# Row maxima of the attention stage: two parts in an even stream of one pair of tiles per half-step, with one VectorE instruction over both heads where their banks are neighbours

## The reference

```
std_attn = softmax(mask(q @ k.T * dh**-0.5))        # "dot" logits, per head
geo_attn = softmax(mask(read_lines @ J_write.T * inc_scale))   # "geo" logits, 6 components per head
combined = (1 - gate) * (std_attn @ v) + gate * (geo_attn @ geo_v)
x = layernorm(x + combined @ out_w + out_b)
x = layernorm(x + down(silu(gate_proj(x)) * up_proj(x)))
```

## Time and profile before

| | |
|---|---|
| median of 3 runs | 1913.83 us (1912.52 to 1914.31) |
| the profiled execution | 1911.92 us, of which span 1910.2 us |
| PE busy | 1686.7 us (88%) |
| ACT busy | 1218.8 us (64%) |
| VectorE (DVE) busy | 1057.9 us (55%), of it 487.9 us in 768 full maxima |
| mean granted TensorE clock | 0.944 of 2.4 GHz |

### The profile page before, as it was taken

How to read it: one execution, slowest core, us unless ns; L and a number is a source line. 1 busy time by engine, 2 the same in 40 slices (tenths; PEclk the granted TensorE clock), 3 DMA queues, 4 the chain that set the end, 5 groups by cost and what they waited for, 6 DMA issues and landing times. The chain is left out here.

```text
span 1910.2 us, 36280 instructions
## 1 busy us (share of the span) xinstructions
PE 1686.7 (88%) x11793; PEld 606.2 (32%) x11793; DVE 1057.9 (55%) x2509; ACT 1218.8 (64%) x1457; POOL 336.5 (18%) x478
## 2 busy tenths in 40 slices
PE   7887469679999999999989999999999874999998
PEld 4544112122222222222222222222222222565555
DVE  4775586355755657556565565755756103545432
ACT  3553308568888788887878878888888861211221
POOL 4432402012111111111111111111110213112000
PEclk9998659889999999999999999999999987999999
DMA  5774511112211111111120111111102004232000
GB/s 170 215 216 145 164 62 41 63 45 77 87 44 67 44 61 73 42 61 57 51 86 34 67 45 59 73 42 62 71 33 68 18 25 152 72 101 97 11 22 22
DMA packets 97400, 140.67 MB, mean 74 GB/s; under 512 B 8144, under 2 KB 66320, under 8 KB 95152
## 3 DMA queue, kind: packets, MB, share of 16 engines
q1 hardware_dynamic: 96000, 135.08, 20.6%
q0 software_dynamic: 624, 2.75, 0.4%
q10 hardware_dynamic: 576, 0.28, 0.1%
HBM read 81.96 MB, written 55.61 MB: 72 GB/s over the span
## 5 line engine op out<-in xcount | busy, mean ns | idle before, releaser
L1074 ACT ACTIVATE prob<-ex 128x1024 f32<-128x1024 f32 (+1 forms) x1152 | 1050.2, 978 | 276.9 <-PE ex L915 256.0
L1101 DVE TENSOR_REDUCE mp<-mx 128x1 f32<-128x512 f32 x768 | 487.9, 685 | 170.2 <-PE mx L943 170.2
L988 PE MATMUL pv<-prob,va 128*32 128x512 f32 (+3 forms) x5120 | 581.1, 545 | 0.6 <-POOL prob L887 0.6
L887 POOL TENSOR_SCALAR_AFFINE_SELECT prob<-prob 128x256 f32<-128x256 f32 (+1 forms) x384 | 186.1, 485 | 1124.1 <-ACT prob L1074 1119.9
L1097 DVE CUSTOM_DVE_ANT_0 dull<-mx,mask_qk 128x128 f32<-128x128 f32 (+3 forms) x512 | 231.5, 487 | 258.1 <-PE mx L943 256.5
L921 PE MATMUL ex<-dq,dk 34*128 34x512 bf16 (+7 forms) x2560 | 344.5, 352 | 29.3 <-ACT prob L1074 28.6
L943 PE MATMUL mx<-dk,dq 64*128 64x512 bf16 (+3 forms) x1280 | 305.0, 363 | 40.4 <-DVE mp L1101 20.5
L915 PE MATMUL ex<-gq,gk 38*128 38x512 bf16 (+3 forms) x1280 | 221.4, 358 | 46.0 <-DMA dq<-mrow 34.4
L915 PEld LDWEIGHTS ex<-gq,gk 38*128 38x128 bf16 x1280 | 57.3, 93 | 440.4 <-ACT prob L1074 368.5
L988 PEld LDWEIGHTS pv<-prob,va 128*32 128x32 f32 x5120 | 115.2, 109 | 227.9 <-issue 191.4
L1427 ACT ACTIVATE sg<-pg 128x512 f32<-128x512 f32 x48 | 28.7, 597 | 246.0 <-PE pg L1367 243.1
(11 more groups left out here) (98 smaller groups left out, 886.8 us busy)
## 6 DMA issues: line engine op xcount, KB each, us to landing
values<-vn SPq DMA_DIRECT2D x32, 512.0 KB, 5.2
va<-values SPq DMA_DIRECT2D x16, 1024.0 KB, 13.3
raw<-on SPq DMA_DIRECT2D x64, 256.0 KB
parts_dot<-sp SPq DMA_DIRECT2D x32, 384.0 KB, 5.0
dq<-parts_dot SPq DMA_DIRECT2D x96, 128.0 KB
dk<-parts_dot SPq DMA_DIRECT2D x96, 128.0 KB
att<-raw SPq DMA_DIRECT2D x32, 256.0 KB
rr<-rden SPq DMA_DIRECT2D x32, 256.0 KB
```

The lines of the kernel that those rows point to most:

```text
L887: g.affine_select(out=cut, in_=cut, compare_op=ALU.is_ge, fill=0.0, base=0, pattern=[[0, nb], [1, P]], channel_multiplier=-1).then_inc(mas ...
L988: last = pe.matmul(pv[blk * VW:(blk + 1) * VW, CH - w:CH], sets[which]["v"][:, kb, blk * VW:(blk + 1) * VW], prob[UNIT_AT[s, j, kind] % NP ...
L1074: act.activation(prob[n % NPROB][:, :].rearrange("p (b c) -> p b c", b=2)[:, :, 0:w], ex[:, n % 2, :].rearrange("p (b c) -> p b c", b=2)[: ...
L1101: last = v.tensor_reduce(out=to, in_=mx[:, t % MX_RING, 0:w], axis=AX.X, op=ALU.max)
```

## The change

The maxima of an item are split into two parts. EARLY holds the query blocks of query tiles 0 to 2 (24 pairs), LATE those of tile 3 (16 pairs). EARLY of item it+1 is computed in h10 to h29 of item it and turned into rows at h30; LATE of item it+1 is computed in h31 to h35 of item it and h0 to h8 of item it+1 itself, and turned at h9 of that item. TensorE waits for the rows of LATE before h21 (`m_in[LATE]`), for those of EARLY at the item's start. Nearly every half-step has one pair, always between the geo and the dot scores; none is put behind the dot scores any more. The narrow diagonal pairs go together: h10 and h31 have three pairs (128, 256, 384 keys), h28 and h29 have two (128 and 256 keys), h9 and h30 none.

A full pair whose two tiles lie in neighbouring banks (0,1 or 1,2) is reduced by one TENSOR_REDUCE over both, which frees both banks at its end: 15 of the 24 full pairs. The pairs in banks 2,0 and all diagonal ones stay as they were.

SP issues the rows of LATE after the second 6 dot loads and before the store of tile 1; each of the 8 DMAs then moves 4 blocks of 256 B (LATE) or 12 (EARLY), where one of before moved 16. The prologue computes EARLY and the first 7 pairs of LATE for item 0; the gates are computed, transposed and copied in it, right after the turn of EARLY, so that `gts_ready` comes before item 0. The last item now has maxima in h0 to h8 and a turn at h9.

The parts of the diff that the text speaks of, in the order SP, TensorE, VectorE behind the layout of the parts:

```diff
+PARTS = ((0, 1, 2), (3,))
+EARLY, LATE = 0, 1
+TURN = (30, 9)
...
+    early = [cuts(0, 0, 1, 2), cuts(0, 3)] + fulls(1) + [cuts(1, 3)] + fulls(2)[0:2] + [cuts(1, 2), cuts(2, 2)]
+    early += fulls(2)[2:] + [cuts(2, 3), cuts(1, 0, 1), cuts(2, 0, 1)]
+    late = [cuts(3, 0, 1, 2)] + fulls(3) + [cuts(3, 3)]
...
             def item(it):
...
+                rows(it, LATE, sets[it % NSET])
                 store(it, 1)
...
                 if it + 1 < ITEMS:
-                    rows(it + 1, sets[(it + 1) % NSET])
+                    rows(it + 1, EARLY, sets[(it + 1) % NSET])
...
-            rows(0, sets[0])
+            rows(0, EARLY, sets[0])
...
                 for j in range(groups):
+                    h = PV_AT[s, j]
+                    to = at if h < LEAD else nxt
                     scores(it, which, s, j, GEO, head)
-                    some(j)
+                    if to:
+                        for u in MAX_IN[h]:
+                            max_pair(it, to, u)
                     scores(it, which, s, j, DOT, head)
-                    if j == groups - 1:
-                        some(groups)
-                    if j == 0 and s == MT_STEP and nxt:
-                        max_rows(nxt)
+                    if to and h in TURN:
+                        turn(it, to, TURN.index(h))
                     earlier(j)
...
-                pe.wait_ge(m_in, (it + 1) * 128)
+                pe.wait_ge(m_in[EARLY], (it + 1) * 128)
                 for s in range(NSTEP):
+                    if s == FIRST_OF[PARTS[LATE][0]]:
+                        pe.wait_ge(m_in[LATE], (it + 1) * 128)
                     step(at, before, nxt, s, head)
...
             def max_pair(it, u):
                 qb, k0, w, on_diagonal = MAXT[u]
+                last, banks = RING.pair(u)
+                if banks and not on_diagonal:
+                    v.wait_ge(mx_ready, RING.ready(it, last))
+                    v.tensor_reduce(out=mp[DOT][:, :, qb, k0 // CH], in_=mx[:, banks, 0:w], axis=AX.X,
+                                    op=ALU.max).then_inc(mx_free, 2)
+                    return
```

More of the change, by code:

```diff
@@ L115 @@
 NTILE = 2 * NMT
-NMX = NTILE + 1
 MX_RING = 3
-MT_STEP = NSTEP - 3
 DEN_STEP = 10
[L122 to L134, removed]
-    return out
@@ L138 @@
[L138 to L149, removed]
+PARTS = ((0, 1, 2), (3,))
+EARLY, LATE = 0, 1
+TURN = (30, 9)
+PART_BLOCKS = [TT * len(qts) for qts in PARTS]
+PART_FIRST = [TT * qts[0] for qts in PARTS]
+PART_OF = [next(p for p in range(2) if qb // TT in PARTS[p]) for qb, _, _, _ in MAXT]
@@ new lines, with __init__, add, ready @@
+MAX_IN = max_places()
+LEAD = TURN[LATE] + 1
+class Ring:
+    def __init__(self):
+        self.order, self.bank, self.tiles, self.part = [], [], [], []
+        at, tiles = 0, 0
+        for h in range(NPV):
+            for u in MAX_IN[h]:
+                for a in range(2):
+                    self.add((u, a), at % MX_RING, tiles, None)
+                    at, tiles = at + 1, tiles + 1
+            for part in range(2):
+                if h == TURN[part]:
+                    self.add(("turn", part), at % MX_RING, None, part)
+                    at += 1 if part == EARLY else 3
+            if h == LEAD - 1:
+                self.head, self.head_tiles = len(self.order), tiles
+        assert tiles == NTILE and at % MX_RING == 0
+        self.uses = len(self.order)
+        self.place = {use: i for i, use in enumerate(self.order)}
+    def add(self, use, bank, tile, part):
+        self.order.append(use)
+        self.bank.append(bank)
+        self.tiles.append(tile)
+        self.part.append(part)
+    def ready(self, it, i):
+        return (it + 1) * self.uses - self.head + i + 1
+    def freed(self, it, i):
+        return (it + 1) * NTILE - self.head_tiles + self.tiles[i] + 1
+    def pair(self, u):
+        first, second = (self.bank[self.place[u, a]] for a in range(2))
+        return self.place[u, 1], slice(first, second + 1) if second > first else None
+    def owner(self, i):
+        j = i - 1
+        while self.bank[j] != self.bank[i]:
+            j -= 1
+        return j % self.uses, j < 0
@@ L152, in set_of, with item_of @@
+RING = Ring()
+EARLY_FIRST = MAX_IN[LEAD][0]
+def item_of(it, part):
+    return it + 1 if part == EARLY else it
 def set_of(k, i):
@@ L959, in wide_pair, with turn @@
                                      start=True, stop=True)
[L960 to L962 removed]
+                last.then_inc(wx_ready[part], 1)
+            def turn(it, to, part):
+                i = RING.place["turn", part]
                 with pe.If(is_wide > 0):
[L964 to L968 removed]
+                    pe.wait_ge(mx_free, RING.freed(it, i - 1))
+                    other = 1 - part
+                    if not (isinstance(it, int) and it < 0):
+                        pe.wait_ge(mrow_ready[other], it + 1)
+                    for n, u in enumerate(PART_TILES[part]):
+                        wide_pair(to, part, n, u)
+                pe.wait_ge(negm_ready[part], to[0] + 1)
+                bank_free(it, i)
+                pe.transpose(mx[:, RING.bank[i], 0:P], negm[part][:, :], ident[:, :]).then_inc(mx_ready, 1)
             def times_v(it, which, use, s, j, head):
```

234 lines of the change are left out of this document (122 added, 112 removed).

## The result

The changed kernel takes 1970.71 us (median of 4 runs, 1969.01 to 1971.38), the one before on the same chip 1913.17 us (1911.44 to 1914.31). The ratio is 1.030, with a 95% interval of 1.028 to 1.032. The direction was the forecast's, the size was not: 1922 was forecast, and 1970.7 lies outside the range. The profiled execution has a span of 1969.6 us and a granted clock of 0.935, against 1910.2 us and 0.944.

A forecast was written before the change was run, and what follows sets the result against it. An item's length was taken to be set by the ScalarE-TensorE round trip, lengthened by pairs behind the dot scores. Terms summed to +8.6 us, 1920.5 profiled; forecast 1922, own range 1911 to 1934, wider range 1887 to 1936.

The forecast's parts named there:

- Gates in the prologue: Before item 1: TensorE's wait for rows goes, -27.4 us, and half clock behind it, -1.2 us.
- A shorter prologue: Start of item 0: EARLY turns sooner, rows wait behind item 1's loads; start at 278.7 instead of 285.73, -7.0 us.
- Rows of LATE behind the dot loads: Before h21: rows land at 1302.8 in item 12, h21 begins 1.5 us later, TensorE idles 2.1 us; 12 items wait.
- Clock: Behind the wait before h21: half of 12 items at half clock, 1.3 us each, +8 us, bounds 0 to +25.
- the clock falls in every item: Rival, chance 0.11: every wait before h21 is followed by half clock, 1930 to 1950 us.
- Diagonal pairs together: Waits for banks: h28 and h29 0.6 us late each, h10 and h31 1.3 us late each, taken whole.
- the narrow pairs hide: Rival, chance 0.19: ScalarE's lead covers the ring's waits, 1.5 to 2.5 us an item back, about 1892 to 1900 us.
- Pairs behind the dot scores that go: Gains per item: 0.6 us each at h6, h13, h17; 0.5 each at h22, h24, h28.
- One instruction over two banks: Full pairs: both banks freed only at its end, priced zero, bounds -0.1 to +0.1 us a half-step where VectorE is late.
- The turn moves from h31 to h30: After h21 in each item: the moved turn was priced as no change.
- Item 15: Last item: LATE pairs, a turn, and waits at h8 (1.9 us) and the turn (0.3 us), together +2.9 us.
- the rows of LATE don't hold up h21: First rival, chance 0.16: rows land before h21, 12 items cost 0.5 instead of 2.6 us, clock stays, 1889 us.

The follow-up runs named there:

- e5: The kernel before with only the gates' transpose and copy moved from the end of item 0 into the prologue: 1880.4 us, ratio 0.983.
- e6: The changed kernel with each operand load of two blocks split into two DMAs of one block: 1887.2 us, ratio 0.987.
- e1: The changed kernel with the 8 DMAs of the LATE rows issued by POOL on its own queue instead of SP: 1915.6 us, ratio 1.002.
- e4: The changed kernel without the branch for unusual inputs at both turns, on TensorE and VectorE: 1947.6 us, ratio 1.019.
- e2: The changed kernel with the triple pairs of h10 and h31 apart, four narrow pairs moved behind dot scores elsewhere: 1950.1 us, ratio 1.017.
- e3: The changed kernel without the instruction over two banks, every tile reduced by its own instruction: 1956.8 us, ratio 1.025.
- e11: e9 without the instruction over two banks, every tile reduced by its own instruction: 1833.6 us, ratio 0.959.
- e9: The changed kernel with both the split loads of e6 and the triple pairs apart as in e2: 1851.6 us, ratio 0.969.
- e10: e9 without the branch for unusual inputs on TensorE and VectorE: 1836.0 us, ratio 0.960.

## Why the prediction was right or wrong

*Gates in the prologue: right.* Item 0 is 28.0 us shorter, and 28.1 in e5, with this edit alone.

*A shorter prologue: right in size.* -7.9 for -7.0, but 1.8 of it stand already ahead of the first maxima, so the prologue itself gave 6.1. Its reason was right as well: in e6, with faster loads, the rows no longer wait. The same prologue is there 4 us shorter; the rest of e6's earlier start comes from `project`.

*Rows of LATE behind the dot loads: the mechanism was right, the term was too small.* Both ways of clearing it (e1, e6) take the whole of h20's +41.1 away. The step that failed is the landing of these rows, the sum 1301.8 + 0.2 + 0.2 + 0.6, and with it the 2.1 us of idle time. Measured from the first exponential of item 12, the last dot load was through 0.8 us later than before and not 0.2 (the store at the head of the queue was issued 0.7 us later), and TensorE went on 1.9 us after the rows' last packet and not 0.6. TensorE itself was 0.4 later than counted. 3.56 us instead of 2.1; over h20 16 us more than foreseen. The 0.6 may fit the prologue of before, in which the rows had an empty queue: there the completions came at the pace of the issues, the last of them 1.15 us after the last issue had ended. Behind the loads all eight were waiting at once, and their completions came one after the other, 1.3 us from first to last. (Item 0 of the earlier trace rows, where rows stood behind other transfers, was the nearer row.) Which items wait was also not quite as foreseen: item 7 did not, and item 8, whose h21 was to be set by the reciprocals, waited 5.5 us for the rows, with which h20 to h24 took it 2.0 us longer than before.

The rule of the Trainium skill ("DMA: Bandwidth & Descriptors", section on why a DMA increments its semaphore by 16) that I weighed there, by which a DMA from SP takes the largest number of engines up to 16 that divides the slowest dimension of both sides, and always the lowest-numbered ones: the trace agrees. Of the rows' 32 packets 16 passed at once and 16 behind the loads, as two free and two busy engines of four would have it, and e6, whose loads have a slowest dimension of 16 or 6 instead of 2, moved 133 GB/s instead of 52 to 57.

*Clock: wrong, and the costliest miss beside the wait.* I counted half of 12 items at 1.3 us each, +8. The rival "the clock falls in every item" (0.11) was nearly it: half clock stands right behind the wait in nine of the items 1 to 14 (it followed eight of the nine waits of 3.3 us or more, and one of 2.69), 115.6 us of the items in all, 48.7 in e6. It also met things that I had priced at full clock: h31 and h32 took 3.3 to 4.2 us more instead of 1.4 to 1.7 in three items. Against e6, which has the same instructions, h21 to h24 are 15 us longer (item 8's own 3 taken off) and h31 and h32 4 us: about 19 us are the clock's. Its row was at 2.5 us of idle time; I had priced the wait at 2.1, and most waits were 3.3 to 3.7. The two misses belong together: of the waits of 3.3 us and more one in nine left the clock at full speed, of the three shorter ones (1.2, 1.8 and 2.7 us) two did.

*Diagonal pairs together: right in mechanism, nearly in size.* h28 and h29 +0.6 each item, counting what left h28 (foreseen +0.7). h10 +1.4 in items 9 to 14 and +1.8 in items 1 to 6, h31 +1.4 to +1.7, for 1.3: over 28 places some 7 us more, the half clock taken off. In e4, without the branch, both are at 1.2 to 1.4 in every item, together 2 us over what was foreseen; so most of that excess goes with the branch and not with the three banks. No shadow covers them, and e2 shows that they were avoidable: both places went back to zero. The rival "the narrow pairs hide" (0.19) is refuted by this.

*Pairs behind the dot scores that go:* h3 to h9 -0.6 and h13 to h19 -1.2 as foreseen; of the 1.0 for h22 and h24 came 0.77, where the clock was full.

*One instruction over two banks, zero: wrong.* e3 is 14 us and e11 18 us faster without it. One part has a known cause: in the prologue VectorE is what is waited for (6.6 us, e11 to e9). I had looked only at the half-steps, where it is not. The other part is no cost of the instruction itself in the wide half-steps (h13 to h19 are at -16.2 with and without it), but of where VectorE stands (next point).

*The turn moves from h31 to h30, no change: wrong.* +8.1 us in items 1 to 7, and VectorE stands another 4.5 us at h1 of items 2, 3, 5 and 6. e4 and e10 show that it goes when the untaken branch goes (-23 and -15.7 us, what follows it included). The Trainium skill ("Advanced Engine Details and Errata", section Control Flow Timing) gives about 108 ns for a compare and branch. Items 9 to 14, with up to 0.21 us where e4 has 0.03, are of that order; items 1 to 7 with 1.8 to 2.1 are far above it. In the kernel before, the same kind of branch, over the code of all 40 pairs, cost VectorE 2.10 us once, in the prologue, and 0.03 to 0.04 us in each of the fifteen turns of the items. That items 1 to 7 have it and 9 to 14 do not, and that removing the two-bank instruction moves it (e3) or ends it (e11), suggests that it depends on how the code lies and not on the work. That is argued and not shown: no run moved code without changing it, and why VectorE stands just there stays open.

*Item 15: right* (+2.2 for +2.9; h8 waited 1.58 us for its bank, 1.9 foreseen).

The first rival, "the rows of LATE don't hold up h21" (0.16), was refuted by the 3.56 us. Its price can now be checked as e1: 1915.6, where I had worked out 1889; most of the 27 us between are the triple pairs (10 over their price), h30 (9) and h21 to h24 (4).

Adding the misses up by the table: h20 +16, h21 to h24 +15, h10 to h12 +6, h31 and h32 +10, h30 and h0 to h2 +10, `finish` +3, less the 8 counted for the clock: 52 us, and small differences the other way take 1 off. That is the distance of the profiled executions, from 1920.5 to 1971.4. Two slips in the prediction's own numbers changed nothing: 1888 stands in one place for the 1889 of the first rival, and -24 to -37 give 1885 to 1898 and not 1892 to 1900 unless part of it is lost to the wait.

## What to carry to other kernels

Before small DMAs on which an engine waits go into a queue, ask what is ahead of them on the engines that they share, and price their landing by a row in which the queue was full; then ask again what the idle time does to the clock, with the upper bound of the wait and not with its middle. How many small DMAs there are may count too: their completions took 0.17 us each here, and no run had fewer of them. Here most of the loss hung on one slow kind of load. Splitting each into two DMAs turned 1970.7 into 1887.2 us, but it gave the kernel before (with its gates moved) 20 us as well: against that measure the change cost 90 us with the slow loads and 27 with the split ones. And a part that is priced at zero in the steady loop should be looked at where the engine that it touches is the bound (here the prologue), and what an untaken branch costs has to be measured.

## What the runs showed of the hardware

- Loads on `[2, n, T]` blocks moved 52 to 57 GB/s while the queue held only them, stores and the rows; the same bytes as two DMAs each moved 133 GB/s in their first 8 us.
- Eight small DMAs whose last packets passed at 1338.5 let TensorE go on at 1340.36, 1.9 us later: their completions came 0.17 to 0.18 us apart. In the prologue of before TensorE started 1.3 us after the last issue had ended.
- TensorE's idle times of 3.3 to 5.6 us before h21 were followed by half clock in eight of nine cases, for 3.4 to 13.7 us; the ninth, of 3.33 us in item 5, was not.
- A reduction over two neighbouring banks takes 1226 ns, two single ones 1.29 us: it saves 5% of VectorE's time, and the first bank is held for 1226 ns and not for some 685.
- VectorE stood 1.8 to 2.1 us before the instruction behind a large branch that was not taken, in seven items of fifteen, and 0.15 to 0.21 us in the others.
